# Fused attention stage: two of the four normalisations move from VectorE to ScalarE

## The reference, cut to what matters

```python
x = x + _layernorm(_L1_attn_ref(_layernorm(x), ...))      # attention without softmax: one matrix per batch
x = x + _layernorm(_L1_ffn_ref(_layernorm(x), ...))       # of this, the stage computes:
#   ln1_out = layernorm(h) * ln1_weight + ln1_bias        -> qkv -> causal attention over the leading axis
#   hidden_after_attn = h + proj(attn)
#   ln2_out = layernorm(hidden_after_attn) * ln2_weight + ln2_bias -> router logits
# layernorm(x) = (x - mean) / sqrt(var + eps)
```

## Time and profile before

| | us |
|---|---|
| median of 3 runs (2459.19 to 2464.46) | 2460.88 |
| the profiled execution | 2457.92 |
| its span, first to last instruction | 2456.2 |
| the fused stage in it | about 1862 to 2065 |
| VectorE busy over the span | 1676.1 (68%) |
| ScalarE busy over the span | 1185.9 (48%) |
| TensorE busy over the span | 1920.1 (78%) |

### The profile page before, as it was taken

How to read it: one execution, slowest core, us unless ns; L and a number is a source line. 1 busy time by engine, 2 the same in 40 slices (tenths; PEclk the granted TensorE clock), 3 DMA queues, 4 the chain that set the end, 5 groups by cost and what they waited for, 6 DMA issues and landing times. The chain is left out here.

```text
span 2456.2 us, 35764 instructions
## 1 busy us (share of the span) xinstructions
PE 1920.1 (78%) x10252; PEld 1469.4 (60%) x10253; DVE 1676.1 (68%) x3193; ACT 1185.9 (48%) x2021; POOL 1483.1 (60%) x1118
## 2 busy tenths in 40 slices
PE   6787878796979787876599999907877784799970
PEld 2445454554555554644499999904655664699970
DVE  1789898989899898985644444436734897644438
ACT  2776767777777767773222222226632441111112
POOL 1799999898989898984133333335622420355532
PEclk9797979797989888887699999958987896799995
DMA  4111111111111010112411111142000014122226
GB/s 125 36 35 40 36 40 35 40 35 41 37 38 38 29 45 31 44 36 82 165 48 47 48 48 47 41 139 77 9 18 11 9 35 163 44 70 70 68 66 191
DMA packets 76781, 138.63 MB, mean 56 GB/s; under 512 B 10370, under 2 KB 47874, under 8 KB 75859
## 3 DMA queue, kind: packets, MB, share of 16 engines
q1 hardware_dynamic: 62994, 99.67, 12.3%
q0 software_dynamic: 13632, 37.24, 4.9%
HBM read 104.86 MB, written 32.01 MB: 56 GB/s over the span
## 5 line engine op out<-in xcount | busy, mean ns | idle before, releaser
L779 DVE TENSOR_TENSOR_SCAN a_hs<-a_dA,a_carry,a_hs 128x512 f32<-128x512 f32 x512 | 628.9, 1267 | 78.2 <-POOL a_hs L396 38.7
L396 POOL TENSOR_TENSOR a_hs<-a_u,a_b_bc 128x1024 f32<-128x1024 f32 x258 | 626.4, 2431 | 0.4
L921 PE MATMUL a_h_ps<-k_ident,a_hs 128*128 128x128 f32 x2064 | 326.6, 307 | 147.1 <-DVE a_acc L742 79.1
L921 PEld LDWEIGHTS a_h_ps<-k_ident,a_hs 128*128 128x128 f32 x2064 | 268.0, 158 | 270.8 <-DVE a_acc L742 75.5
L551 ACT ACTIVATE a_dA<-a_delta,a_a_neg 128x512 f32<-128x512 f32 x512 | 350.8, 688 | 31.2 <-DVE a_hs L779 29.3
L408 POOL TENSOR_TENSOR a_acc<-a_acc,a_part 128x512 f32<-128x512 f32 x242 | 317.7, 1313 | 59.7 <-ACT a_part L565 58.7
L565 ACT ACTIVATE a_part<-a_h_ps,a_c_tok 128x512 f32<-128x512 f32 x242 | 165.9, 686 | 193.6 <-PE a_h_ps L921 186.4
L1221 POOL DMA_INDIRECT expert_rows<-m0e_ys,k_pair x71 | 79.1, 1114 | 232.4 <-DVE m0e_ys L1277 217.9
L855 PE MATMUL a_fx<-a_hT,a_w_x 128*128 128x512 f32 x432 | 201.9, 599 | 2.2 <-ACT a_halo L487 1.4
L742 DVE SCALAR_TENSOR_TENSOR a_acc<-a_h_ps,a_c_tok,a_acc 128x512 f32<-128x512 f32 x242 | 176.1, 728 | 30.7 <-PE a_h_ps L921 30.7
L1287 DVE TENSOR_TENSOR m0e_hT<-m0e_gs,m0e_u 128x512 f32<-128x512 f32 x70 | 48.2, 689 | 190.9 <-ACT m0e_gs L1240 190.9
(11 more groups left out here) (420 smaller groups left out, 3793.2 us busy)
## 6 DMA issues: line engine op xcount, KB each, us to landing
a_b_bc<-b_rows SPq DMA_DIRECT2D x132, 256.0 KB, 3.1
c_y<-expert_rows SPq DMA_DIRECT2D x16, 512.0 KB, 5.7
q_y<-expert_rows SPq DMA_DIRECT2D x16, 512.0 KB, 5.9
norm_rows<-a_x SPq DMA_DIRECT2D x9, 512.0 KB, 3.2
m0w_up<-in_m_up SPq DMA_DIRECT2D x1, 4096.0 KB, 12.5
m0w_gate<-in_m_gate SPq DMA_DIRECT2D x1, 4096.0 KB, 22.4
m0w_down<-in_m_down SPq DMA_DIRECT2D x1, 4096.0 KB, 31.9
c_xl<-in_L_attn_x SPq DMA_DIRECT2D x8, 512.0 KB, 3.5
```

The source lines that it names most:

```text
L396: pool.tensor_tensor(hs[n % NBUF][:, half, :], u[s][:, half, :], b_bc[:, n % NBUF:n % NBUF + 1, :].broadcast_to([P, 2, T]), ALU.mult).then ...
L779: dve.tensor_tensor_scan(hs[k][:, c, :], dA[c][:], hs[k][:, c, :], carry[:, hf, c, n:n + 1], ALU.mult, ALU.add).then_inc(s_scan, 1)
L921: last = pe.transpose(hT_ps[j % 2][:, c * P:(c + 1) * P], hs[(n - 1) % NBUF][:, c, j * P:(j + 1) * P], ident[:])
```

## The change

The eight instructions that make n2 of unit k and n1 of unit p + 1 leave VectorE. ScalarE makes them in the same turn, right behind the two `qkv` copies and ahead of `p_attT`, as `Identity` with a scale of 1/sqrt(var + eps) and a bias of -mean/sqrt(var + eps). GpSimd makes that bias: per unit, two 128x4 instructions for n1 (`x_neg`, `x_sh`) and two for n2 (`h_neg`, `h_sh`), behind the powers. VectorE's `a4` gets a wait on `s_fin`. Nothing else moves.

```diff
 # GpSimd
-                    pool.tensor_tensor(RS2[:, :, U * Q:(U + 1) * Q], x_v[U % 2][:, 1], half2, ALU.pow).then_inc(s_fin, 1)
+                    pool.tensor_tensor(RS2[:, :, t], x_v[U % 2][:, 1], half2, ALU.pow).then_inc(s_xp, 1)
+                    pool.tensor_scalar(x_neg[:], MVv[:, :, t, 0], -1.0, None, ALU.mult).then_inc(s_xp, 1)
+                    pool.wait_ge(s_xp, 3 * (U + 1))
+                    pool.tensor_tensor(x_sh[U % 2][:], RS2[:, :, t], x_neg[:], ALU.mult).then_inc(s_fin, 1)
...
 # ScalarE
+            def normal(out, U, src, rstd, shift):
+                for q, t in enumerate(tiles(U)):
+                    last = act.activation(out[:, q, :], src[:, t, :], ACT.Identity, scale=rstd[:, t:t + 1],
+                                          bias=shift[:, q // Q, q % Q:q % Q + 1])
+                return last
...
                         act.activation(qkv[p % 2][:, q, :], q_ps[q][:], ACT.Copy).then_inc(s_qc, 1)
+                if has(k):
+                    act.wait_ge(s_r2, k + 1)
+                    if k >= 2:
+                        act.wait_ge(s_rst[k % 2], 32 * (k // 2))
+                    normal(n2[k % 2], k, per.H, per.R2, h_sh[k % 2]).then_inc(s_n2, 1)
+                if has(p + 1):
+                    act.wait_ge(s_fin, p + 2)
+                    normal(n1[(p + 1) % 2], p + 1, x, per.RS2, x_sh[(p + 1) % 2]).then_inc(s_n, 1)
...
 # VectorE
-                if has(k):
-                    dve.wait_ge(s_r2, k + 1)
-                    if k >= 2:
-                        dve.wait_ge(s_rst[k % 2], 32 * (k // 2))
-                    normal(n2[k % 2], k, per.H, per.MV2, per.R2).then_inc(s_n2, 1)
-                if has(p + 1):
-                    dve.wait_ge(s_fin, p + 2)
-                    normal(n1[(p + 1) % 2], p + 1, x, per.MV, per.RS2).then_inc(s_n, 1)
```

More of the change, by code:

```diff
@@ L2006, in attend_phase @@
         x_v = [m.sb(f"x_v{s}", [P, 2, B, Q]) for s in range(2)]
+        x_neg = m.sb("x_neg", [P, B, Q])
+        x_sh = [m.sb(f"x_sh{s}", [P, B, Q]) for s in range(2)]
+        h_neg = m.sb("h_neg", [P, B, Q])
+        h_sh = [m.sb(f"h_sh{s}", [P, B, Q]) for s in range(2)]
         n1 = [m.sb(f"n1{s}", [P, 2 * Q, D]) for s in range(2)]
@@ L2046, in attend_phase @@
         s_v2 = m.sem("x_stats")
+        s_xp = m.sem("x_powers")
         s_fin = m.sem("x_scale")
@@ L2057, in attend_phase @@
         s_hv = m.sem("hidden_stats")
+        s_hp = m.sem("hidden_powers")
         s_r2 = m.sem("hidden_scale")
@@ L2104, in _ @@
             R2 = per.R2[:].rearrange("p (b t) -> p b t", b=B)
+            MVv = per.MV[:].rearrange("p (b t) v -> p b t v", b=B)
+            MV2v = per.MV2[:].rearrange("p (b t) v -> p b t v", b=B)
             pool.wait_ge(s_rowc, B)
@@ L2121, in _ @@
                     pool.wait_ge(s_v2, U + 1)
-                    pool.tensor_tensor(RS[:, :, U * Q:(U + 1) * Q], x_v[U % 2][:, 0], half2, ALU.pow)
-                    pool.tensor_tensor(RS2[:, :, U * Q:(U + 1) * Q], x_v[U % 2][:, 1], half2, ALU.pow).then_inc(s_fin, 1)
+                    if U:
+                        pool.wait_ge(s_fin, U)
+                    t = slice(U * Q, (U + 1) * Q)
+                    pool.tensor_tensor(RS[:, :, t], x_v[U % 2][:, 0], half2, ALU.pow).then_inc(s_xp, 1)
+                    pool.tensor_tensor(RS2[:, :, t], x_v[U % 2][:, 1], half2, ALU.pow).then_inc(s_xp, 1)
+                    pool.tensor_scalar(x_neg[:], MVv[:, :, t, 0], -1.0, None, ALU.mult).then_inc(s_xp, 1)
+                    pool.wait_ge(s_xp, 3 * (U + 1))
+                    pool.tensor_tensor(x_sh[U % 2][:], RS2[:, :, t], x_neg[:], ALU.mult).then_inc(s_fin, 1)
                 if has(n) and has(n - LATE_P - 1):
@@ L2132, in _ @@
                     pool.wait_ge(s_hv, U + 1)
-                    pool.tensor_tensor(R2[:, :, U * Q:(U + 1) * Q], h_v[U % 2][:], half2, ALU.pow).then_inc(s_r2, 1)
+                    if U:
+                        pool.wait_ge(s_r2, U)
+                    t = slice(U * Q, (U + 1) * Q)
+                    pool.tensor_tensor(R2[:, :, t], h_v[U % 2][:], half2, ALU.pow).then_inc(s_hp, 1)
+                    pool.tensor_scalar(h_neg[:], MV2v[:, :, t, 0], -1.0, None, ALU.mult).then_inc(s_hp, 1)
+                    pool.wait_ge(s_hp, 2 * (U + 1))
+                    pool.tensor_tensor(h_sh[U % 2][:], R2[:, :, t], h_neg[:], ALU.mult).then_inc(s_r2, 1)
         @block.scalar
@@ L2319, in _ @@
                 if has(o):
+                    dve.wait_ge(s_fin, o + 1)
                     c_a4 = mark(normal(a4, o, x, per.MV, per.RS))
```

## The result

| | before | changed |
|---|---|---|
| median, us | 2460.03 (4 runs) | 2483.08 (4 runs, 2479.97 to 2484.46) |
| ratio | | 1.0091, interval 1.0077 to 1.0105 |
| profiled execution; span | 2457.92; 2456.2 | 2482.0; 2480.3 |

What follows compares the result with a forecast made beforehand. Prediction: VectorE looks like the bound, but a second loop through ScalarE and TensorE is almost as long. Turn terms, from late start, 3.94 us ScalarE work and clock, sum to +22.4 on 2460.9: 2483.3 us, range 2467 to 2491.

Steps and rivals of the forecast that it cites:

- the whole 3.94 us falls on the second loop: Ahead of `p_attT`: eight ScalarE instructions, 3.94 us, unhidden on the loop through ScalarE and TensorE from exponential to exponential.
- 2.0 us of clock for a wait of 4.3 us: Turns 5 to 9: TensorE's clock falls while waiting for `p_attT`, slowing n2's transposes and projection by 2.0 us (ends 1.6, 3.0).
- The clock terms of turns 4 and 10: TensorE's shorter waits for `p_attT`, at least 2 and 2.4 us, also lower its clock: 1.5 and 1.6 us.
- The first turns: Turns 0 to 3: VectorE, relieved of two groups of four, reaches turn 3's products earlier: -2.6 us (ends 0, -3.4).
- The last turn: Turn 12: last n2 alone on the path, ScalarE +0.7 and two small GpSimd instructions +0.5: +1.2 us.
- Rival A: TensorE's clock stays up in turns 4 to 10: without clock loss the sum drops to +9.3 us, 2470; chance 0.18.
- Rival B: At `k_hidden`, turns 4 to 10: VectorE is the true bound, ScalarE's work fits its idle half; about 2440 us; chance 0.05.

Runs made afterwards that it cites:

- e1: Changed kernel with ScalarE making each of n1 and n2 a second time into unused tiles, right behind the first; median 2510.0 us, ratio 1.022 to the kernel before.
- e2: Changed kernel with TensorE doing matmuls whose results are overwritten while it waits for the attention copy in turns 5 to 10; ratio 1.0042 to the kernel before.
- e4: Changed kernel with n2 made ahead of the qkv copies and n1 last before the exponential, both still on ScalarE; ratio 0.9964 to the kernel before.
- e8: Kernel before with only n1 moved to ScalarE, last before the exponential; n2 stays on VectorE; ratio 0.9951 to the kernel before.
- e9: Kernel before with n1 on ScalarE, last before the exponential, and n2 on ScalarE ahead of the qkv copies in turns 5 to 7 only; 2445.96 us, ratio 0.9939.
- e5: Changed kernel with n1 made last before the exponential; n2 stays between the qkv copies and the attention copy; ratio 1.0013 to the kernel before.
- e3: Changed kernel with n1 and n2 back on VectorE; GpSimd's bias instructions and VectorE's extra wait stay; ratio 1.0006 to the kernel before.
- e11: e4 with eight extra calls of matmul on TensorE, results overwritten, in turn 8's long wait; ratio 0.9952 to the kernel before.
- e10: e9 with eight extra calls of matmul on TensorE, results overwritten, in turn 8's long wait; ratio 0.9953 to the kernel before.

## Why the prediction was right, point by point

| turns | forecast | measured |
|---|---|---|
| first (0 to 3) | -2.6 | -1.8 |
| 4 | +1.5 | +0.35 |
| 5 | -1.1 | -1.55 |
| 6 | +4.4 | +4.05 |
| 7 | +3.5 | +4.06 |
| 8 | +5.3 | +5.23 |
| 9 | +6.5 | +7.78 |
| 10 | +3.7 | +3.74 |
| last (11, 12) | +1.2 | +1.9 |
| sum | +22.4 | +23.8 |

- The step "the whole 3.94 us falls on the second loop": shown. e1 added it again, e2 left it bare at the forecast turn lengths (21.84 for 21.87 in turn 6, 17.23 for 17.26 in turn 9), e4 took it away by place alone.
- "2.0 us of clock for a wait of 4.3 us": measured 1.7, 1.7, 2.6, 1.9 in turns 5 to 8. Right in mechanism and nearly in size.
- The clock terms of turns 4 and 10 (1.5 and 1.6) were wrong as placed: waits of 2.78 and 2.34 us were followed by full speed in the changed kernel. Two losses I had not listed took their place: the `qkv` matmuls of turns 9 and 10 ran slow, 1.7 us each, behind a wait of 1.21 us that before had done nothing. So turn 9 came out 1.3 above, turn 4 1.15 below, and turn 10 right for the wrong reason. The clock terms added up to 13.1 us and measured 12.8 in e2, with errors of both signs: the size of their sum is partly luck.
- The first turns gained 1.8 instead of 2.6. The gain itself is n1's: the kernels with n1 on ScalarE have 57.1 or 55.7 us there, those with n1 on VectorE 58.9 or 61.3. What lies between 57.1 and 55.7 is clock: the first group of L2399 took 2.96 us in the changed kernel and 1.89 in e4. So -1.8 or -3.2, around the forecast, and both hold some 0.6 us of GpSimd's new instructions, which the prediction had put at nothing there: in turn 1 the row addition behind them starts 2.6 us after the powers in e4 and in the changed kernel, and 2.05 before.
- The last turn: +1.9 for +1.2. ScalarE's four instructions and GpSimd's bias cost what was said; the rest is the projection of turn 11 at 4.36 us instead of 3.70.
- Rival A (clock up) did not come about, but had the right price for what lies under the clock: +9.3 forecast, +10 measured in e2. Rival B is refuted where it stood, by VectorE's 5.02 us wait; but e4, e8 and e9, 9 to 15 us faster than before, show what it was right in: relieving VectorE pays once ScalarE's part is off the loop.

## What to carry to other kernels

Moving work from an engine that is 95% busy to one that is 50% busy helps only if the new place is one where that engine waits; in a fixed order, look for the idle time in brackets and put the work right ahead of it, and never ahead of the instruction for which a third engine waits. When two loops are within a few per cent of each other, work out the length of the second one before unloading the first. If TensorE waits behind the new work, add the clock to its price.

## What the runs showed of the hardware that was not expected

- A wait's length does not by itself decide TensorE's clock. Behind the same 2.34 us the eight transposes and the projection took 1.94 and 4.29 us in one turn of e5 and 1.06 and 3.62 in the next; behind 2.4 us in turn 7 they were slow before and fast in e3; in e11 a turn's first `qkv` group took 2.90 us behind a wait of 1.21 us, and 1.53 behind the same wait one turn earlier. From these rows a single clock loss behind waits of 1.2 to 2.8 us can be forecast only as a chance; over turns 4 to 10 the errors had both signs and the sum came out within 0.2 us.
- 16 filling matmuls in a wait of 4.3 us (8 in the shorter wait of turn 10) left the transposes and the projection behind them at full speed in all six turns of e2, with a granted clock of 1.00 in five (0.91 in turn 8, whose `qkv` group ran slow ahead of the filler), and shortened the kernel by 12 us, though they compute nothing. The same 16 in e10 gained nothing: behind matmuls at full speed and a wait of only 0.71 us they themselves ran at a granted clock of 0.58.
- The two small GpSimd instructions of 128x4 took mostly 0.20 to 0.23 us each, like its other multiplication (0.20), and up to 0.37 us in the changed kernel.

Why the `qkv` matmuls are slow in turn 9 and fast in turn 10 in e4, and the other way round in e11, behind equal waits, stays open.
